# Attention heads 2 to 7 of a graph network: the greater of two exponents on VectorE, one exponential instead of two on ScalarE, and the means on ScalarE

## What is computed

```python
h = (x @ W.T).reshape(n, heads, out_ch)
a_src = jnp.einsum('nhc,hc->nh', h, att_src)
a_dst = jnp.einsum('nhc,hc->nh', h, att_dst)
e = a_src[src] + a_dst[dst]
e = jax.nn.leaky_relu(e, NEG_SLOPE)          # NEG_SLOPE = 0.2
m = jax.ops.segment_max(e, dst, num_segments=n)
ex = jnp.exp(e - m[dst])
denom = jax.ops.segment_sum(ex, dst, num_segments=n)
alpha = ex / (denom[dst] + EPS)
msg = alpha[:, :, None] * h[src]
out = jax.ops.segment_sum(msg, dst, num_segments=n)
```

## Time and profile before

| | |
|---|---|
| median of 3 runs | 1759.04 us (1754.56 to 1760.23) |
| profiled execution | 1759.04 us, span 1757.3 us |
| PE busy | 1692.5 us, 96% |
| DVE busy | 933.1 us, 53% |
| ACT busy | 463.1 us, 26% |
| POOL busy | 693.0 us, 39% |
| mean granted TensorE clock | 0.983 of full speed |

### The profile page before, as it was taken

The page is one execution under the profiler, slowest core; times in us unless marked ns, Lnnn a source line. Parts: engine busy times, 40 slices in busy tenths (PEclk is TensorE's granted clock), DMA queues, the critical chain, the costliest instruction groups (busy, mean ns, idle before and its releaser), DMA issues.

```text
span 1757.3 us, 25860 instructions
## 1 busy us (share of the span) xinstructions
PE 1692.5 (96%) x10227; PEld 1587.7 (90%) x10227; DVE 933.1 (53%) x1879; ACT 463.1 (26%) x875; POOL 693.0 (39%) x428
## 2 busy tenths in 40 slices
PE   8799999999999988899899999999999999999999
PEld 7699999997999988899377788989999999998999
DVE  8993446417865679957497554423112141235731
ACT  6444123203222138924223211101011011112320
POOL 1026855552445531051020075532644434342654
PEclk9899999999999999899899999999999999999999
DMA  2002221323111210014010021111211111110212
GB/s 89 1 28 73 74 72 63 136 74 126 63 55 60 68 55 10 1 46 140 8 43 1 1 90 60 61 48 37 73 63 54 47 53 59 50 54 29 73 63 71
DMA packets 41999, 99.83 MB, mean 57 GB/s; under 512 B 10508, under 2 KB 12142, under 8 KB 41894
## 3 DMA queue, kind: packets, MB, share of 16 engines
q1 hardware_dynamic: 37828, 87.87, 15.7%
q10 hardware_dynamic: 4066, 10.46, 1.7%
HBM read 96.39 MB, written 1.92 MB: 56 GB/s over the span
## 4 chain that ended last, share of the span: by engine, by line
PE 81%; DVE 11%; ACT 4%; POOL 2%; issue 1%; POOLq 0%; DVEq 0%; ACTq 0%
PE bank L2396 10%; PE bank L2398 10%; PE bank L2397 10%; PE banks L2396 9%; PE banks L2397 9%; PE banks L2398 9%; PE bank L2959 3%; PE banks L2959 3%; PE bank L3036 3%; PE bank L3041 3%; PE banks L3036 2%; PE banks L3041 2%; DVE src_hot L1469 1%; DVE tmp L1803 1%; PE banks L2811 1%
## 5 line engine op out<-in xcount | busy, mean ns | idle before, releaser
L823 POOL TENSOR_TENSOR w_hi<-raw,ones_r 128x768 fp32r<-128x768 f32 (+1 forms) x192 | 294.5, 1534 | 1009.6 <-PE banks L2398 369.5
L826 POOL TENSOR_TENSOR w_lo<-raw,w_hi 128x768 fp32r<-128x768 f32 (+1 forms) x192 | 372.8, 1941 | 15.1
L2396 PE MATMUL bank<-w_hi,xT_hi 128*125 128x384 f32 (+2 forms) x560 | 188.6, 337 | 2.3 <-DVE small L1943 1.2
L2398 PE MATMUL bank<-w_hi,xT_lo 128*125 128x384 f32 (+2 forms) x560 | 187.3, 334 | 0.0
L2397 PE MATMUL bank<-w_lo,xT_hi 128*125 128x384 f32 (+2 forms) x560 | 187.2, 334 | 0.0
L2396 PE MATMUL banks<-w_hi,xT_hi 128*125 128x384 f32 (+2 forms) x440 | 151.7, 345 | 0.0
L2397 PE MATMUL banks<-w_lo,xT_hi 128*125 128x384 f32 (+2 forms) x440 | 151.4, 344 | 0.0
L2398 PE MATMUL banks<-w_hi,xT_lo 128*125 128x384 f32 (+2 forms) x440 | 151.3, 344 | 0.0
L1594 DVE TENSOR_TENSOR hT_lo<-tmp,hT_hi 128x312 fp32r<-128x312 f32 (+1 forms) x88 | 92.1, 1051 | 42.4 <-ACT hT_hi L966 42.0
L2396 PEld LDWEIGHTS bank<-w_hi,xT_hi 128*125 128x125 f32 x560 | 104.6, 187 | 5.9 <-POOL w_lo L826 1.5
L2397 PEld LDWEIGHTS bank<-w_lo,xT_hi 128*125 128x125 f32 x560 | 104.6, 187 | 2.5
(11 more groups left out here) (579 smaller groups left out, 3937.7 us busy)
## 6 DMA issues: line engine op xcount, KB each, us to landing
raw<-wa SPq DMA_DIRECT2D x92, 384.0 KB, 3.0
raw<-wc SPq DMA_DIRECT2D x76, 384.0 KB, 3.0
raw<-wb SPq DMA_DIRECT2D x28, 448.0 KB, 3.3
w_rows<-w_in ACTq DMA_DIRECT2D x1, 3072.0 KB, 12.8
bias<-bias_in ACTq DMA_DIRECT2D x6, 384.0 KB
w_first<-w_in ACTq DMA_DIRECT2D x1, 2304.0 KB, 9.1
w_down<-w_down_in SPq DMA_DIRECT2D x8, 288.0 KB, 5.3
w_up<-w_up_in SPq DMA_DIRECT2D x1, 2304.0 KB, 10.8
```

The lines of the kernel that those rows point to most:

```text
L823: pool.tensor_tensor(w_hi[:, k, 0:width], raw[:, k, 0:width], ones[:, 0:1].to_broadcast([P, width]), ALU.mult).then_inc(S("unit_high"), 1)
L826: pool.tensor_tensor(w_lo[:, k, 0:width], raw[:, k, 0:width], f(w_hi[:, k, 0:width]), ALU.subtract).then_inc(S("unit_split"), 1)
L2396: tell_used(pe.matmul(dst, l_hi, r_hi, start=start, stop=False))
L2398: return pe.matmul(dst, l_lo, r_hi, start=False, stop=stop)
```

## The change

For heads 2 to 7 VectorE first takes the greater of the two exponents, straight from both halves of `uB` (new line 1993; the constant `a_max` is now the difference of the two branches' source terms, made once at new line 2055). ScalarE makes one exponential in place in `prob` (new line 1140), and VectorE limits it and multiplies by `adj` (new line 2025). The division is no longer two instructions of VectorE, but five of ScalarE, one for each target tile, with the reciprocal as scale (`head_mean` on ScalarE, new line 1194). `head_low` of heads 0 to 3 moves into the weights of heads 4 to 7, and that of heads 4 to 7 behind the last sums. Copies into `uB` wait for VectorE's last read of the buffer; the products' banks become free by ScalarE's reads.

```diff
--- before.py
+++ after.py
@@ -315,7 +315,8 @@
         if h + 2 < HEADS:
             pairs("g2p_uvB", 4 * (h + 2), 4)
         if h < HEADS:
-            several_from("g2p_agg", 2 * h, 2, "g2p_mean")
+            add("g2p_agg", 2 * h, "g2p_mean", NT * h + 3)
+            add("g2p_agg", 2 * h + 1, "g2p_mean", NT * h + NT)
         if h == 0:
             pairs("g2p_uvT", 2)
         if 0 < h < HEADS:
@@ -1123,6 +1124,8 @@
                                    ).then_inc(S(layer + "_uvT_read"), 1)
 
             def shifts(layer, h):
+                if layer == "g2q" or h >= 4:
+                    act.wait_ge(*E("g2p_greater", NT * (HEADS if layer == "g2q" else h - 1)))
                 for i in range(4):
                     c0, cn = CH[i % 2]
                     await_group(act, layer + "_uvB", 4 * h + i)
@@ -1132,11 +1135,14 @@
             def powers(layer, h, s):
 
                 made = NT * h + s
+                if layer == "g2p" and h >= 2:
+                    act.wait_ge(*E("g2p_greater", made + 1))
+                    act.activation(prob_of(layer, h)[:, s], prob_of(layer, h)[:, s], ACT.Exp,
+                                   bias=a_src5[0:TN, 8 * s + h:8 * s + h + 1]).then_inc(S("g2p_powers"), 1)
+                    return
                 if s == 0:
                     act.wait_ge(*E(layer + "_uvB_read", 4 * h + 4))
                     act.wait_ge(*E(layer + "_fifth", 1))
-                    if h >= 4:
-                        await_group(act, "g2p_agg", 2 * (h - 2) + 1)
                 if made >= 3:
                     act.wait_ge(*E(layer + "_greater", made - 2))
                 act.activation(prob_of(layer, h)[:, s], uB_of(layer, h)[:, 0], ACT.Exp, bias=a_cols[0:TN, 16 * s + h:16 * s + h + 1])
@@ -1177,14 +1183,29 @@
                 act.wait_ge(*E("g2p_relu", 2 * h + 2))
                 act.activation(hT_hi[:, h, 0:NODES], head_T[:], ACT.Copy).then_inc(S("g2p_high"), 1)
 
+            def head_mean(h):
+
+                act.wait_ge(*E("g2p_sum", 3 * h + 3))
+                if h >= 2:
+                    await_group(act, "g2p_outT", 2 * (h - 2) + 1)
+                for n in range(NT):
+                    i, at = (0, n) if n < 3 else (1, n - 3)
+                    await_group(act, "g2p_agg", 2 * h + i)
+                    act.activation(mean[:, h % 2, n], bank("g2p_agg", 2 * h + i)[0:TN, at * (HEAD_DIM + 1):
+                                                                                 at * (HEAD_DIM + 1) + HEAD_DIM],
+                                   ACT.Copy, scale=prob8[0:TN, NT * h + n:NT * h + n + 1]).then_inc(S("g2p_mean"), 1)
+
             powers("g2p", 1, NT - 1)
             for h in range(2, HEADS + 3):
                 if h < HEADS:
                     shifts("g2p", h)
                     if h == 2:
                         shift_rows("g2p", 1)
+                        head_mean(0)
                     for s in range(NT):
                         powers("g2p", h, s)
+                if h <= HEADS:
+                    head_mean(h - 1)
                 if h >= 3:
                     head_out(h - 3)
 
@@ -1964,6 +1985,14 @@
             def greater_branch(layer, h, s):
 
                 pr, made = prob_of(layer, h), NT * h + s
+                if layer == "g2p" and h >= 2:
+                    if s == 0:
+                        dve.wait_ge(*E("g2p_uvB_read", 4 * h + 4))
+                        if h >= 4:
+                            await_group(dve, "g2p_agg", 2 * (h - 2) + 1)
+                    STT(pr[:, s], uB_of(layer, h)[:, 0], a_max[0:TN, 8 * s + h:8 * s + h + 1], uB_of(layer, h)[:, 1],
+                        ALU.add, ALU.max).then_inc(S("g2p_greater"), 1)
+                    return
                 dve.wait_ge(*E(layer + "_powers", made + 1))
                 STT(pr[:, s], pr[:, s], 3.0, lesser[:, made % 3], ALU.min, ALU.max).then_inc(S(layer + "_greater"), 1)
 
@@ -1982,6 +2011,20 @@
                             await_group(dve, "g2p_asB", 2 * other + 1)
                         greatest_score("g2p", other, d)
 
+            def weights_of_head(h):
+
+                pr = prob_of("g2p", h)
+                for s in range(NT + 1):
+                    if s < NT:
+                        greater_branch("g2p", h, s)
+                    for a, b in PARTS:
+                        if s == b + 1 or (s == NT and b == NT):
+                            if b == NT and h >= 4:
+                                head_low(h - 4)
+                            dve.wait_ge(*E("g2p_powers", NT * h + b))
+                            STT(pr[:, a:b], pr[:, a:b], 3.0, f(adj[:, a:b]), ALU.min, ALU.mult
+                                ).then_inc(S("g2p_prob"), 1)
+
             def weights_of_last():
 
                 pr = prob[0]
@@ -2008,6 +2051,8 @@
             weights_of_edges(0, [(h, d) for h in range(HEADS - 2, HEADS) for d in range(NT)])
             shift_parts("g2p", 1, HEADS)
             weights_of_edges(1)
+            dve.wait_ge(*E("g2p_uv", 2))
+            link(TT(v8(a_max), scores[:, :, 0], v8(a_src5), ALU.subtract))
 
             def head_mean(h):
 
@@ -2022,14 +2067,8 @@
                 for i, (a, b) in enumerate(parts):
                     await_group(dve, "g2p_agg", 2 * h + i)
                     TS(total[:, a:b], sums(i)[:, :, HEAD_DIM], 1e-16, None, ALU.add).then_inc(S("g2p_sum"), 1)
-                dve.wait_ge(*E("g2p_sum", 2 * h + 2))
-                link(dve.reciprocal(total, total))
-                if h >= 2:
-                    await_group(dve, "g2p_outT", 2 * (h - 2) + 1)
-                for i, (a, b) in enumerate(parts):
-                    TT(mean[:, h % 2, a:b], sums(i)[:, :, 0:HEAD_DIM],
-                       total[:, a:b].unsqueeze(2).to_broadcast([TN, b - a, HEAD_DIM]), ALU.mult
-                       ).then_inc(S("g2p_mean"), 1)
+                dve.wait_ge(*E("g2p_sum", 3 * h + 2))
+                dve.reciprocal(total, total).then_inc(S("g2p_sum"), 1)
 
             def head_low(h):
                 dve.wait_ge(*E("g2p_high", h + 1))
@@ -2037,14 +2076,15 @@
 
             for h in range(HEADS + 3):
                 if 1 < h < HEADS:
-                    weights_of_edges(h)
+                    weights_of_head(h)
                 if 1 <= h <= HEADS:
                     head_mean(h - 1)
                 if h == 3:
                     for half in (hT_hi, hT_lo):
                         dve.memset(f(half[:, 0:HEADS, NODES:NP]), 0.0).then_inc(S("hT_pads"), 1)
-                if h >= 3:
-                    head_low(h - 3)
+                if h >= HEADS:
+                    for ended in range(HEADS - 4 if h == HEADS else h - 3, h - 2):
+                        head_low(ended)
 
             dve.wait_ge(*E("g2_xn", NT))
             dve.wait_ge(*E("g2_bias_full", 16))
@@ -2815,7 +2855,7 @@
             def turn_head(h):
 
                 for i, (a, b) in enumerate(((0, 4), (4, NT))):
-                    pe.wait_ge(*E("g2p_mean", 2 * h + 2))
+                    pe.wait_ge(*E("g2p_mean", NT * h + NT))
                     dst = open_bank("g2p_outT", 2 * h + i)
                     for n in range(a, b):
                         last = pe.transpose(dst[:, (n - a) * TN:(n - a + 1) * TN], mean[:, h % 2, n], ident[0:TN, 0:TN])
```

## The result

| | median | runs | ratio to before, 95% interval |
|---|---|---|---|
| before | 1759.28 us | 4 (1754.56 to 1760.23) | |
| changed | 1774.49 us | 4 (1773.09 to 1775.90) | 1.0089 (1.0075 to 1.0104) |

The change makes the kernel 15.2 us slower; 1771.6 (1765 to 1779) was predicted. The profiled execution of the changed kernel took 1775.9 us, its span is 1774.2. It was the longest of the four.

A forecast was written before the change was run, and what follows sets the result against it. TensorE was taken to bound the kernel (busy 96%), ScalarE the heads' stage. 11.4 us at the last product plus 1.2 at the end gave 12.6: span 1757.3 to 1769.9, with 1.7 around it 1771.6 us, range 1765 to 1779.

The forecast's parts named there:

- The circle.: Heads' rounds: VectorE's reciprocal, then ScalarE's means, head_out and copies, then VectorE's next maximum, in turn; 12.8 us against 10.07.
- The maximum's price: VectorE's maxima in the heads' rounds: new form with a column operand taken at the old cost, one step 0.72 us.
- The means: Five small ScalarE instructions a head, dividing by the sums: 1.4 us together, floor 0.9, ceiling 1.77.
- If the means take over 0.35 each, that term is: Sign for the profile after: ScalarE's five divisions per head over 0.35 us each would show their term mis-sized.
- TensorE in the circle.: Heads' products start only at the round's turn, behind the copies; delay 0.1 us or so a round, ceiling 1.1.
- longer by TensorE: Rival for the heads' rounds: half clock lasts through each product, 2 to 5 us more, 1774 to 1777; chance 0.13.
- "The sum": last product: Head 7's weights, which TensorE's last product awaits: done at 760.05 instead of 748.71 us, 11.4 later.
- the wait of 4 to 4.5 us ahead of the first maximum: Sign on VectorE: first maximum of a round idle that long behind ScalarE's copies, five times.
- The same last product (6.99).: TensorE's last product behind head 7's weights keeps its length of 6.99 us.
- The end (+1.2).: Before the score rows, TensorE waits 0.7 to 1.6 us for the last low part; 1.2 taken, floor nothing.
- The chain I named: Behind the last weights: means 1.4 us, then three times head_out and low part, 7.6 together, to the score rows.
- Absorbed: Rival behind the heads: TensorE would wait after 760 us for weights anyway, end stays at 1759; chance 0.02.

The follow-up runs named there:

- copies first, divisions on VectorE: Changed kernel with divisions back on VectorE, ScalarE's next-head copies right behind the exponentials, low parts of heads 4 and 5 before the last sums: 1756.59 us.
- divisions on VectorE: Changed kernel with the divisions back on VectorE as two instructions and no means on ScalarE: 1759.97 us, ratio 1.0012.
- order at the end: Changed kernel with head_out(5) ahead of head 7's means on ScalarE and head 4's low part ahead of the last sums on VectorE: 1774.12 us.

## Why the prediction was right

The direction and the mechanism were right, and the time lies in the range; two terms of the sum were too small (last product by 1.8 us, the end by 2.5) and one too large (the length of the last product, by 1.7), and that they partly cancel is luck. The sum was 12.6 us, 15.2 were measured.

- **"The circle."** Right. From 727.13 to 740.20, beside what was predicted: VectorE up to the reciprocal's end 8.73 (8.40), hand-over 0.03 (0.03), means 1.27 (1.4), `head_out` 1.62 (1.57), copies to the next maximum 1.42 (1.41). Sum 13.07 (12.8). That it is a circle, and that order alone makes it, is shown by three orders of ScalarE's list, with the same instructions: 13.07, 11.49 and 8.69 us.
- **The maximum's price** is the mis-sized term in it: "I take the new form at the same". It takes 0.865 us, not 0.81, and its like follows at 0.78 instead of 0.72: 0.3 us a round, about 1.6 over the stage.
- **The means** were near. "If the means take over 0.35 each, that term is" mis-sized was badly put: they take 0.371, but overlap by more than I took, so five are 1.27 to the start of the next instruction. By the figures of the Trainium skill (ScalarE: Activation LUTs, "What ACT_TABLE_LOAD costs") the estimate is 386 ns for one and 1.56 us for five; the trace has 371 ns and 1.40 us, a little less.
- **"TensorE in the circle."** Right that it would be close. The products of heads 2 to 6 start right behind the copies and begin at half the clock; one round was longer by 0.16. The rival "longer by TensorE" did not come true.
- **"The sum": last product.** +13.1 us instead of +11.4. Head 2's round took 11.44 (11.25), the others 13.07, 13.07, 13.07 and 13.23 (12.8). Of the signs, the wait of 4 to 4.5 us ahead of the first maximum came four times and not five: head 3's, with no `head_out` ahead of it, was 2.76, as its own sum had it.
- **The same last product (6.99).** Wrong: it took 5.32, 1.7 less. What differs is the clock: before, it is at half from 749 to 752 (0.50), now at full from 761 on. TensorE waited only 1.06 us before it instead of 2.17. But it also took 5.32 behind a gap of 2.57 us (copies first, divisions on VectorE), and 6.99 behind 3.01 (divisions on VectorE), so the gap in front alone doesn't set it. The clock goes with the length there too (1.00 throughout, and 0.50 from 748 to 751); what sets the clock stays open.
- **The end (+1.2).** This step failed. I followed only the chain of low parts to the score rows, and began it with `head_out(5)` right behind the means, though that waits for the low part of head 4, which now stands behind the last reciprocal. What holds first are two banks of PSUM that `head_out` of heads 5 and 6 reads: TensorE waits 2.07 and 1.20 us for them, and the way from the end of the last product to the score rows is 3.7 us longer. At the score rows themselves nothing waits. The chain I named is real, but by the profiles lies 1.6 us under the banks ("order at the end").
- 13.1 - 1.7 + 3.7 = 15.2 with the decimals kept: so much later do the score rows start (779.70 and 764.51), and so large is the difference of the medians. In the profiled execution a stretch at half the clock near 856 us adds 1.6 (spans 16.9 apart); the others are 0.8 to 2.8 us shorter than it. **Absorbed** was wrong: nothing behind 780 us gives the delay back.

Groups by form of the changed kernel, for these two terms (count, busy us, mean ns of one, idle time ahead and its releasers):

```profile
L1993 DVE SCALAR_TENSOR_TENSOR prob<-uB,small 125x626 f32<-125x626 f32 x30 | 24.4, 865 | 20.1 <-ACT uB L1132 11.4 <-PE bank L2786 8.7
...
L1194 ACT ACTIVATE mean<-banks,small 125x128 f32<-125x128 f32 x32 | 9.0, 371 | 15.3 <-DVE small L2071 12.9 <-PE banks L2861 2.5
```

The 20.1 us of idle time ahead of the maxima are the circle's price on VectorE, the 12.9 ahead of the means what ScalarE stands for the reciprocals.

## What to carry to other kernels

Where work goes over to another engine, look at what it waits for and what stands behind it in that engine's list before counting busy time: an instruction that waits for the end of a round must not stand ahead of one that starts the next. When one circle is open, look for the next, through banks that are read late. Here the order of the same instructions alone made 1774, 1764, 1762 or 1750 us.

## What the runs showed of the hardware

- A maximum on VectorE of 125x626 whose scalar is a column in SBUF takes 0.865 us and follows its like at 0.78; with a constant in that place it was 0.81 and 0.72. The kernels differ in the operation too (addition and maximum, against minimum and maximum), and no run tells the two apart.
- A low part (128x625) on VectorE takes 0.80 us in the stage of the heads, where GpSimd is idle. Behind it, in the changed kernel, it takes 1.97 and 2.09 us while GpSimd splits weights, 0.81 in GpSimd's pause between 772.7 and 777.3, and 1.60 after it (timeline below); before, the longest was 1.61.

```profile
767.51 1.97 DVE L2075 TENSOR_TENSOR hT_lo<-head_T,hT_hi 128x625 fp32r<-128x625 f32 x1
771.30 2.09 DVE L2075 TENSOR_TENSOR hT_lo<-head_T,hT_hi 128x625 fp32r<-128x625 f32 x1 [1.82 <-ACT hT_hi L1184]
775.22 0.81 DVE L2075 TENSOR_TENSOR hT_lo<-head_T,hT_hi 128x625 fp32r<-128x625 f32 x1 [1.82 <-ACT hT_hi L1184]
...
770.88 1.85 POOL L827 TENSOR_TENSOR w_lo<-raw,w_hi 128x768 fp32r<-128x768 f32 x1
777.32 1.47 POOL L824 TENSOR_TENSOR w_hi<-raw,ones_r 128x768 fp32r<-128x768 f32 x1 [4.59 <-PE banks L2438]
```

These are the timelines of VectorE and of GpSimd. No run took GpSimd's work away, so the cause is read from the trace, not shown.
